# Gate logits as eight more columns of the value and output products, and a new order of the last attention steps

## The chip, the cores and the metric

The kernel runs on one core of a Trainium2 chip. The metric is the device time of one execution in microseconds. Lower is better. Nothing else runs on the chip.

## The reference

The block is linear attention followed by a mixture of experts, both on layer-normed rows with a residual. There are 4 batches of 1024 tokens, 512 features, 16 heads of 32, 8 experts with a hidden width of 2048, and each token goes to its best two experts.

```python
xn = layernorm(x)
q, k, v = xn @ q_w.T + q_b, xn @ k_w.T + k_b, xn @ v_w.T + v_b      # per head
qp, kp = elu(q) + 1, elu(k) + 1
attn = (qp @ (kp.T @ v)) / (qp @ kp.sum(tokens) + 1e-6)
x1 = x + attn @ o_w.T + o_b
x1n = layernorm(x1)
gates = softmax(x1n @ gating_w)           # 8 logits of each token
top two experts of each token, a position in each expert (cumulative count), capacity 1280
out = x1 + sum over the two experts of weight * (relu(row @ w1 + b1) @ w2 + b2)
```

## The kernel before

One core does all. The program has an attention stage, which also routes the tokens to experts, and then an expert stage. The change touches the attention stage and its seam with the first expert.

**Precision.** Most matrix products are made of three matmuls of type fp32r: both operands are split in a rounded part (`_hi`, by ACT) and a rest (`_lo`, by DVE), and hi·hi, lo·hi and hi·lo are summed. One product of a 128-row tile with a 512x512 matrix is 4 chunks of 3 matmuls of 512 columns (`product`, lines 1290 to 1300). Transposes, the gate logits, the sums over heads and the counts are plain f32 matmuls.

**Tiles and steps.** The 4096 tokens are 32 tiles of 128 rows. Every engine walks the same list of steps `t`, and step `t` works on several tiles at different stages: V and K products on tile t-3, key-value accumulation (KV) on t-4, a quarter of a query product (Q) on t-6, sums over heads (NUM) on t-13, the transpose of the attention rows (A) on t-14, the output product (O) on t-15, the transpose of the second normed rows (N) and the gate logits (L) on t-16. So steps 16 to 34 hold everything, steps 35 to 47 hold fewer and fewer parts, and from step 38 on there is neither V, K nor Q. The order of the parts within a step is written out by hand, apart for each engine: there is no scheduler. An engine that waits in its list holds up all that stands behind it.

**PE** in a full step: V, (counts of a batch, in one step of eight), transpose of xn, O, N, K, A, L, NUM, KV, Q.

**DVE** in a full step: xt_lo, (state of a batch, in one step of eight: `kvb`, `kvd`), `residual` (x1 = product + xr, its statistics), keys, at_lo, `normalize_x1` (x1n), keys_mapped, `attention` (division, writes `at`), xn and its statistics, a piece of routing in six steps of eight, queries_mapped.

**ACT** copies PSUM out (vx, the _hi parts, nt) and does the exponentials. **POOL** does the small steps of the norms (`norm_scale`: add, power), adds the output bias to the residual rows (xr) and scatters routing records to a table in DRAM, 4 indirect DMAs in a step, four steps for a batch. **SP** issues loads and stores in order; `store_rows(v)` waits for x1 and then for x1n of a tile.

**The gate logits** come from x1n: N transposes x1n, ACT copies it to `nt`, L multiplies by the 512x8 gate matrix, and `read_logits` copies the logits of 8 tiles. `route_logits`, `route_gates`, `route_choices` then choose experts; `cnt` goes to PE (`counts`), which gives positions.

**The seam.** At step 36 SP issues the eight 512 KB loads of the first expert's w1. POOL gathers the first expert's rows (`xg`) once two batches are scattered (EARLY_TABLE), PE transposes them (`rows_turned_early`), and `first_layer(0, 0, s)` starts in the last steps. first_layer(0, 0, 2) is the first matmul work behind the last step.

Of the kernel before, what the change touches and what calls it, by code (L numbers as in the profile page):

```python
# [13 lines left out]
F32 = mybir.dt.float32  # L14
# [17 lines left out]
def moe_block(nc, x_in, wq_t, bq, wk_t, bk, wv_t, bv, wo_t, bo, gate_w, w1, b1, w2, b2, out):  # L32
# [3 lines left out]
    NT = S // P  # L36
    KC = D // P
# [11 lines left out]
    ROUTE_STEPS = 36 + NT  # L49
# [14 lines left out]
    with ctx:  # L64
# [7 lines left out]
        bank = [ctx.enter_context(nc.psum_tensor(f"bank{i}", [P, 512], F32)) for i in range(8)]  # L72
# [25 lines left out]
        for c in "kv":  # L98
            whi[c], wlo[c] = sa(f"w{c}_hi", [P, KC, D], F32R), sa(f"w{c}_lo", [P, KC, D], F32R)
# [13 lines left out]
        whi["o"], wlo["o"] = sa("wo_hi", [P, KC, D], F32R), sa("wo_lo", [P, KC, D], F32R)  # L113
# [9 lines left out]
        nt = sa("nt", [P, KC, P])  # L123
# [6 lines left out]
        gw = sa("gw", [P, KC, E])  # L130
        stats = sa("stats", [P, 2, 6])
        mv = sa("mv", [P, 2, 2])
        ve = sa("ve", [P, 2])
        rstd = sa("rstd", [P, 2])
        stats2 = sa("stats2", [P, 6])
        mv2 = sa("mv2", [P, 2])
        ve2 = sa("ve2", [P, 1])
        rstd2 = sa("rstd2", [P, 1])
# [43 lines left out]
        v_full, v_done = n_("v_full"), n_("v_done")  # L182
# [9 lines left out]
        nt_full, nt_done = n_("nt_full"), n_("nt_done")  # L192
        lg_full = n_("lg_full")
        route = n_("route")
        lg_exp_in, lg_exp, lg_read = n_("lg_exp_in"), n_("lg_exp"), n_("lg_read")
# [14 lines left out]
        NTILES = B * NT  # L210
        W = P + HPG
        Z0 = 3 * R
# [11 lines left out]
        LAST_KEYS = NTILES + VK - OUT  # L224
# [18 lines left out]
        def logit_bank(b):  # L243

            return bank[5] if b < B - 1 else bank[3]

        def out_bank(v):

            return bank[7] if v < LAST_KEYS else bank[2] if v < NTILES - NT else bank[4]

# [80 lines left out]
        def _(sp):  # L331
# [36 lines left out]
            load_x(0)  # L368
            load_matrix(0, wv_t)
# [6 lines left out]
            sp.dma_start(gw[:], gate_w.rearrange("(c p) e -> p c e", p=P)).then_inc(small_landed, 16)  # L376
            with nc.allow_non_contiguous_dma(reason="512 biases"):
                sp.dma_start(bqt[:], bq.rearrange("(c p) -> p c", p=P)).then_inc(small_landed, 16)
# [67 lines left out]
        def _(pool):  # L446
# [25 lines left out]
            def norm_scale(v, done, var, tmp_, out_, step_done, ready):  # L472

                pool.wait_ge(done, v + 1)
                nc.gpsimd.tensor_scalar(tmp_, var, LN_EPS, None, ALU.add).then_inc(step_done, 1)  # L475
                pool.wait_ge(step_done, v + 1)
                nc.gpsimd.tensor_tensor(out_, tmp_, nhalf[:], ALU.pow).then_inc(ready, 1)

# [60 lines left out]
            for t in range(STEPS):  # L539
# [8 lines left out]
                if v is not None:  # L548
                    norm_scale(v, mv2_done, mv2[:, 1:2], ve2[:], rstd2[:], ve2_done, rstd2_done)
# [7 lines left out]
                if v is not None:  # L557
                    norm_scale(v, mv_done, mv[:, v % 2, 1:2], ve[:, v % 2:v % 2 + 1], rstd[:, v % 2:v % 2 + 1],
                               ve_done, rstd_done)
# [5 lines left out]
                if t == EARLY_TABLE + 1:  # L565
                    pool.wait_ge(kv_acc, NTILES)
# [47 lines left out]
        def _(act):  # L614
            def matrix_hi(m):

                for half in range(2):
                    act.wait_ge(st_landed[2 * (m % 2) + half], 16 * (m // 2 + 1))
                    nc.scalar.activation(whi[MATRICES[m]][:, 2 * half:2 * half + 2, :], matrix_half(m, half), ACT.Copy) \
# [77 lines left out]

            for t in range(STEPS):
# [5 lines left out]
                if v is not None:  # L704
                    act.wait_ge(v_full, v + 1)
                    if v >= 2:
                        act.wait_ge(kv_acc, v - 1)
                    nc.scalar.activation(vx[:, v % 2, :, 0:P], bank[2][:].rearrange("p (g c) -> p g c", g=G), ACT.Copy) \
                        .then_inc(v_done, 1)
                v = tile_at(t, TURN_X)  # L710
                if v is not None:
# [3 lines left out]
                    split_hi(bank[0], xt_hi[:, :, P * (v % NT):P * (v % NT + 1)], xt_hi_done)  # L715
                for m_ in range(KC):
# [833 lines left out]
```

## Time and profile before

| | |
|---|---|
| median of 3 runs | 2082.67 us (2082.58 to 2087.34) |
| the profiled execution | 2085.72 us |
| its span | 2084.0 us |
| PE busy | 2021.5 us, 97% |
| DVE / ACT / POOL busy | 929.9 / 598.0 / 417.3 us |
| mean granted TensorE clock | 0.99 |

The page's busy shares are averages over two stages. The attention stage ends at about 535 us of the span; the rest is the expert stage, which the change leaves as it is. The durations of single matmuls in the timeline are latencies (390 ns for 512 columns): what a matmul costs in a dense stretch is the distance from its start to the next one's.

### The profile page before, as it was taken

To read this page: it belongs to the slowest core of one execution; us is meant where nothing else is said; L and a number is where in the kernel's file an instruction comes from. 1 tells how busy PE (TensorE), PEld (TensorE's weight loads), DVE (VectorE), ACT (ScalarE), POOL (GpSimd) and SP (SyncE) were. 2 spreads that over 40 slices of the span, in tenths; PEclk is the share of its full clock that TensorE was granted. 3 is DMA by queue.
4 is the path that set the end of the run, shared out by engine and by line. 5 is a ranking of instruction groups with operands and counts; after the bars stand their busy time and mean duration, and the time that the engine had idled before them with its cause. 6 is when DMAs were issued, how large, how long until landed. Compare 5 with 4: busy or idle time off the path is not lost.

```text
span 2084.0 us, 28871 instructions
## 1 busy us (share of the span) xinstructions
PE 2021.5 (97%) x10128; PEld 1754.1 (84%) x10129; DVE 929.9 (45%) x1768; ACT 598.0 (29%) x890; POOL 417.3 (20%) x472
## 2 busy tenths in 40 slices
PE   8999999987999989999999999999999999999996
PEld 7788888876789989998998878889988988888895
DVE  5455557566842452345333432353234334334332
ACT  4333333321331341234122322232123123223221
POOL 1021113335621210221122021121120120220221
PEclk9999999998999999999999999999999999999998
DMA  7112122154202440244023321431143242232221
GB/s 199 58 58 75 64 79 72 47 172 124 75 22 41 130 98 20 40 111 116 20 40 91 101 55 19 126 87 24 32 111 96 40 110 91 45 100 92 55 40 20
DMA packets 114875, 156.05 MB, mean 75 GB/s; under 512 B 28032, under 2 KB 60928, under 8 KB 114816
## 3 DMA queue, kind: packets, MB, share of 16 engines
q1 hardware_dynamic: 93216, 112.13, 17.3%
q0 software_dynamic: 21600, 43.16, 11.5%
q8 instruction: 34, 0.56, 0.1%
q14 instruction: 25, 0.20, 0.0%
HBM read 113.15 MB, written 42.10 MB: 74 GB/s over the span
## 4 chain that ended last, share of the span: by engine, by line
PE 90%; DVE 3%; issue 2%; ACT 2%; POOL 1%; DMA 1%; SPq 1%; ACTq 0%; DVEq 0%; POOLq 0%
PE bank L1297 28%; PE bank L1299 28%; PE bank L1298 28%; PE bank L1316 2%; PE bank L1305 2%; PE bank L1482 1%; PE bank L1470 1%; PE bank L1457 1%; POOL slot_table L528 0%; SPq L385 0%; DMA xr<-_attn_hidden_states_dram 0%; DVE w_lo L838 0%; ACT w_hi L629 0%; ACT ys L646 0%; DMA xb<-_attn_hidden_states_dram 0%
## 5 line engine op out<-in xcount | busy, mean ns | idle before, releaser
L864 DVE CAST h_hi<-h 128x512 fp32r<-128x512 f32 x320 | 138.7, 433 | 846.9 <-ACT h L659 834.5
L659 ACT ACTIVATE h<-bank,b_cur 128x512 f32<-128x512 f32 x320 | 220.2, 688 | 997.6 <-PE bank L1299 965.7
L1297 PE MATMUL bank<-et_hi,w_hi 128*128 128x384 f32 (+1 forms) x1280 | 456.6, 357 | 14.6 <-issue 8.9
L1299 PE MATMUL bank<-et_hi,w_lo 128*128 128x384 f32 (+1 forms) x1280 | 455.6, 356 | 0.0
L1298 PE MATMUL bank<-et_lo,w_hi 128*128 128x384 f32 (+1 forms) x1280 | 454.4, 355 | 0.0
L1299 PE MATMUL bank<-w_hi,h_lo 128*128 128x512 f32 x1072 | 420.8, 393 | 0.0
L1297 PE MATMUL bank<-w_hi,h_hi 128*128 128x512 f32 x1072 | 420.5, 392 | 0.0
L1298 PE MATMUL bank<-w_lo,h_hi 128*128 128x512 f32 x1072 | 420.1, 392 | 0.0
L514 POOL DMA_INDIRECT out_dram<-ys,tab_s x80 | 129.1, 1613 | 1027.5 <-ACT ys L646 1009.2
L1297 PEld LDWEIGHTS bank<-et_hi,w_hi 128*128 128x128 f32 x1280 | 241.1, 188 | 43.5 <-issue 9.9
L1298 PEld LDWEIGHTS bank<-et_lo,w_hi 128*128 128x128 f32 x1280 | 240.9, 188 | 25.2 <-issue 0.2
L1299 PEld LDWEIGHTS bank<-et_hi,w_lo 128*128 128x128 f32 x1280 | 240.7, 188 | 17.5
L1299 PEld LDWEIGHTS bank<-w_hi,h_lo 128*128 128x128 f32 x1072 | 201.1, 188 | 42.7
L1298 PEld LDWEIGHTS bank<-w_lo,h_hi 128*128 128x128 f32 x1072 | 201.3, 188 | 36.8
L1297 PEld LDWEIGHTS bank<-w_hi,h_hi 128*128 128x128 f32 x1072 | 201.4, 188 | 35.8
L866 DVE TENSOR_TENSOR h_lo<-h,h_hi 128x512 fp32r<-128x512 f32 x320 | 222.1, 694 | 11.0
L496 POOL DMA_INDIRECT xg<-normed,tab_g x80 | 81.1, 1013 | 66.3 <-DMA tab_g<-slot_table 48.2
L838 DVE TENSOR_TENSOR w_lo<-w_raw,w_hi 128x1024 fp32r<-128x1024 f32 x64 | 78.0, 1219 | 3.4 <-ACT w_hi L629 3.4
L475 POOL TENSOR_SCALAR ve<-mv 128x1 f32<-128x1 f32 x64 | 14.4, 225 | 324.0 <-DVE mv L917 192.2
L844 DVE TENSOR_TENSOR w_lo<-w_raw,w_hi 128x1024 fp32r<-128x1024 f32 x64 | 78.0, 1219 | 0.0
L528 POOL DMA_INDIRECT slot_table<-rec,slot_i x64 | 72.2, 1128 | 27.6 <-issue 18.3
L850 DVE TENSOR_TENSOR et_lo<-bank,et_hi 128x512 fp32r<-128x512 f32 x84 | 54.0, 684 | 44.4 <-ACT et_hi L641 44.4
(190 smaller groups left out, 2222.9 us busy)
## 6 DMA issues: line engine op xcount, KB each, us to landing
w_raw<-L_ffn_w_dram SPq DMA_DIRECT2D x128, 512.0 KB, 3.7
xb<-_attn_hidden_states_dram SPq DMA_DIRECT2D x32, 256.0 KB, 2.7
xr<-_attn_hidden_states_dram SPq DMA_DIRECT2D x32, 256.0 KB
out_dram<-x SPq DMA_DIRECT2D x32, 256.0 KB
normed<-x1n SPq DMA_DIRECT2D x32, 256.0 KB
normed<-zrow SPq DMA_DIRECT2D x1, 2048.0 KB, 8.3
out_dram<-zrow SPq DMA_DIRECT2D x1, 2048.0 KB, 12.9
b_cur<-L_ffn_b_dram SPq DMA_DIRECT2D x8, 256.0 KB
```

The lines of the kernel that those rows point to most:

```text
L496: nc.gpsimd.indirect_dma_start(out=xg[:, h, :], out_offset=None, in_=normed, in_offset=bass.IndirectOffsetOnAxis(ap=tab_g[:, h, 0:1].bitca ...
L514: nc.gpsimd.indirect_dma_start(out=out, out_offset=bass.IndirectOffsetOnAxis(ap=tab_s[:, h, 0:1].bitcast(I32), axis=0), in_=ys[:, h, :], i ...
L528: nc.gpsimd.indirect_dma_start(out=table, out_offset=bass.IndirectOffsetOnAxis(ap=slot_i[:, c, i:i + 1], axis=0), in_=rec[:, c, i, :], in_ ...
L659: nc.scalar.activation(h32[:, mm % 2, :], h_bank[mm % 2][:], ACT.Relu, bias=b1_cur[:, mm:mm + 1]) \
L838: ve_.tensor_tensor(w1_lo[:, :, cols], w1_raw[:, :, cols], w1_hi[:, :, cols].bitcast(F32), ALU.subtract).then_inc(w1_ready, 1)
L844: ve_.tensor_tensor(w2_lo[:, two, :], w2_raw[:, two, :], w2_hi[:, two, :].bitcast(F32), ALU.subtract).then_inc(w2_ready, 1)
L850: ve_.tensor_tensor(et_lo[:, k, :], src[:], et_hi[:, k, :].bitcast(F32), ALU.subtract) \
L864: ve_.tensor_copy(h_hi[:, mm % 4, :], h32[:, mm % 2, :]).then_inc(h_split_hi, 1)
L866: ve_.tensor_tensor(h_lo[:, mm % 4, :], h32[:, mm % 2, :], h_hi[:, mm % 4, :].bitcast(F32), ALU.subtract).then_inc(h_ready, 1)
L1297: mm_(out_, lh, rh, start=(first and c == 0), stop=False)
L1298: mm_(out_, lh, rl, start=False, stop=False)
L1299: ins = mm_(out_, ll, rh, start=False, stop=(last and c == n - 1))
```

## The change

1. **V product.** The value matrix gets 8 more columns, the gate matrix. The 520 output columns lie across two PSUM banks, so each product is done as two: 268 columns and 252 columns. The second part shares its bank with the KV sums and accumulates on zeros, which ACT writes after each tile. On one step of eight PE waits for `kvb` between the two parts.
2. **O product.** Its first part shares a bank with the other half of the KV sums, so it too waits for `kvb`; where V stands ahead of it in the step, V has waited already, and only step 36 has O and a new `kvb` without V. The output matrix gets 8 columns (o_w.T times the gate matrix, worked out once on the chip in steps 9 to 11 by 16 transposes and 20 small products), 252 and 268 columns.
3. **Logits.** DVE adds the two sets of 8 columns (`lgs`), and `route_logits` corrects for mean and scale of the second norm with 5 more operations in each batch. N, the copy `nt`, L and `read_logits` go.
4. **x1n** is made by ACT instead of DVE, behind its other work of the step; POOL makes one more small operation for it and one for `std`.
5. **Order.** There is one step less; the routing steps come one step earlier. From step 37 (TAIL) on PE does NUM, A, O, and DVE does attention, at_lo, residual. `state` and `read_counts` stand at the front of DVE's step. Clearing `xg` moves from POOL to ACT.

The diff, cut to its core:

```diff
-        STATS, NORM, TURN_X, VK, KV, QUERY = 0, 1, 2, 3, 4, 6
-        RESIDUAL, NUM, TURN_A, OUT, TURN_N, LOGIT = 13, 13, 14, 15, 16, 16
-        ROUTE = NT + LOGIT
-        STEPS = NTILES + LOGIT
+        V0, O0 = 244, 260
+        KV0 = (254, 0)
+        RESIDUAL, NUM, TURN_A, OUT = 13, 13, 14, 15
+        ROUTE = NT + OUT
+        STEPS = NTILES + OUT
+        TAIL = NTILES + KV + 1
+        FRESH = TAIL - OUT
+        GATES = 9
...
 # POOL
+                    nc.gpsimd.tensor_scalar(shift2[:, one], mv2[:, v, 0:1], rstd2[:, one], -1.0, ALU.mult, ALU.mult) \
+                        .then_inc(shift2_done, 1)
...
-                    nc.gpsimd.memset(xg[:], 0.0).then_inc(xg_cleared, 1)
...
 # ACT
+            def normalize_x1(v):
+
+                act.wait_ge(shift2_done, v + 1)
+                if v >= 2:
+                    act.wait_ge(x1n_stored[v % 2], 16 * (v // 2))
+                nc.scalar.activation(x1n[:, v % 2, :], x1[:, v % 2, :], ACT.Identity, scale=rstd2[:, v:v + 1],
+                                     bias=shift2[:, v:v + 1]).then_inc(x1n_done, 1)
...
+                    nc.scalar.activation(lgx[:, v, :], pair_v[:, V0 + D:V0 + DE], ACT.Copy).then_inc(v_read, 1)
+                    act.wait_ge(v_read, v + 1)
+                    nc.scalar.activation(pair_v[:, 512:V0 + DE], zrow[:, 0:V0 + DE - 512], ACT.Copy).then_inc(v_done, 1)
...
-                    nc.scalar.activation(nt[:], bank[0][:].rearrange("p (c t) -> p c t", c=KC), ACT.Copy).then_inc(nt_done, 1)
...
 # DVE, residual
-                ve_.tensor_tensor(x1[:, v % 2, :], out_bank(v)[:], xr[:, v % RRING, :], ALU.add).then_inc(x1_done, 1)
+                ve_.tensor_tensor(x1[:, v % 2, :], pair_o[:, O0:O0 + D], xr[:, v % RRING, :], ALU.add).then_inc(x1_done, 1)
+                dve.wait_ge(std_done, v + 1)
+                ve_.scalar_tensor_tensor(out=lgs[:, v, :], in0=lgx[:, v, :], scalar=std[:, v:v + 1],
+                                         in1=pair_o[:, O0 + D:O0 + DE], op0=ALU.mult, op1=ALU.add).then_inc(lgs_done, 1)
...
 # PE
-                    product(bank[2][:], rows_, lambda k: (whi["v"][:, k, :], wlo["v"][:, k, :]), KC,
-                            matrix=0 if v == 0 else None).then_inc(v_full, 1)
+                    product(pair_v[:, V0:512], rows_,
+                            lambda k: (whi["v"][:, k, 0:512 - V0], wlo["v"][:, k, 0:512 - V0]), KC,
+                            matrix=0 if v == 0 else None)
...
+                    b = batch_at(t, KVD)
+                    if b is not None:
+                        pe.wait_ge(kvb_done, G * (b + 1))
...
+                    product(pair_v[:, 512:V0 + DE], rows_,
+                            lambda k: (whi["v"][:, k, 512 - V0:DE], wlo["v"][:, k, 512 - V0:DE]), KC, first=False,
+                            shared=True).then_inc(v_full, 1)
...
+                    if t >= KVD:
+                        pe.wait_ge(kvb_done, G * min(B, (t - KVD) // NT + 1))
+                    pe.wait_ge(at_done, min(NTILES - NT, t - NUM + (1 if t >= TAIL else 0)))
...
+                    product(pair_o[:, O0:512], out_rows,
+                            lambda k: (whi["o"][:, k, 0:512 - O0], wlo["o"][:, k, 0:512 - O0]), KC, first=(v >= FRESH),
+                            shared=True)
+                    product(pair_o[:, 512:O0 + DE], out_rows,
+                            lambda k: (whi["o"][:, k, 512 - O0:DE], wlo["o"][:, k, 512 - O0:DE]), KC).then_inc(o_full, 1)
...
-                    turn(bank[0], x1n[:, v % 2, :]).then_inc(nt_full, 1)
...
-                    for k in range(KC):
-                        ins = mm_(logit_bank(b)[:, E * i:E * (i + 1)], nt[:, k, :], gw[:, k, :], start=(k == 0),
-                                  stop=(k == KC - 1))
```

Three places show what moves. First PE around the third batch's counts, step 42 into 43 before:

```order
1667 L1298 MATMUL bank<-wo_lo,at_hi 128x512
1668 L1299 MATMUL bank<-wo_hi,at_lo 128x512
1669 L1305 MATMUL bank<-ident,x1n 128x128 x4
1670 L1305 MATMUL bank<-ident,at 128x128 x4
1671 L1457 MATMUL bank<-gw,nt 128x8 x4
1672 L1470 MATMUL bank<-kvd,qp 128x132 x4
1673 L1372 MATMUL bank<-cnt,upper 128x64
1674 L1373 MATMUL bank<-cnt,ones 128x64
1675 L1297 MATMUL bank<-wo_hi,at_hi 128x512
```

and now, step 41 into 42:

```order
2377 L1370 MATMUL pair_o<-wo_lo,at_hi 128x268
2378 L1371 MATMUL pair_o<-wo_hi,at_lo 128x268
2379 L1444 MATMUL bank<-cnt,upper 128x64
2380 L1445 MATMUL bank<-cnt,ones 128x64
2381 L1493 MATMUL bank<-kvd,qp 128x132 x3
2382 L1493 MATMUL pair_v<-kvd,qp 128x132
2383 L1377 MATMUL bank<-ident,at 128x128 x4
2384 L1369 MATMUL pair_o<-wo_hi,at_hi 128x252
```

The transposes of x1n and the logits are gone, and the counts stand directly behind the O product of the step whose choices they count.

Second DVE at the state of the second batch (step 20), before:

```order
209 L985 SCALAR_TENSOR_TENSOR qp<-bank,bq_one,qe 128x512
210 L832 TENSOR_TENSOR xt_lo<-bank,xt_hi 128x4x128
211 L924 COPY ks<-bank 128x2 x2
212 L927 SCALAR_TENSOR_TENSOR kvb<-bvb,ks,bank 128x128 x4
213 L934 TENSOR_TENSOR kvd<-kvb,headmask 128x4x128
```

and now:

```order
222 L1041 SCALAR_TENSOR_TENSOR qp<-bank,bq_one,qe 128x512
223 L985 COPY ks<-pair_v 128x2
224 L985 COPY ks<-pair_o 128x2
225 L988 SCALAR_TENSOR_TENSOR kvb<-bvb,ks,pair_v 128x128 x2
226 L988 SCALAR_TENSOR_TENSOR kvb<-bvb,ks,pair_o 128x128 x2
227 L995 TENSOR_TENSOR kvd<-kvb,headmask 128x4x128
```

`kvb` moved ahead of xt_lo, behind the queries of the step before; PE now waits for it in the middle of V.

Third ACT in steps 40 to 43, as it stands now (x1n is what moved here from DVE, gt is the exponential of the gates):

```order
322 L660 ACTIVATE w_hi<-w_raw 128x4x256
323 L746 ACTIVATE gt<-gt 128x64
324 L656 ACTIVATE at_hi<-bank 128x512
325 L739 ACTIVATE x1n<-x,shift,rstd 128x512
326 L656 ACTIVATE at_hi<-bank 128x512
327 L739 ACTIVATE x1n<-x,shift,rstd 128x512
```

Each at_hi, the split of a later tile's attention rows, stands behind the x1n of an earlier tile, which waits for DVE's statistics and POOL.

## Rows read from the trace of the kernel before

**Rows 1.** The page: busy time of the engines.

```profile
PE 2021.5 (97%) x10128; PEld 1754.1 (84%) x10129; DVE 929.9 (45%) x1768; ACT 598.0 (29%) x890; POOL 417.3 (20%) x472
```

**Rows 2.** Windows of the attention stage; the first row names the columns.

```profile
core 0: us, PE busy (x) PEld busy (x) DVE busy (x) ACT busy (x) POOL busy (x), PEclk, DMA share, GB/s
...
250.00:300.00 50.00, 50.00 (x283) 42.88 (x282) 27.73 (x64) 15.38 (x27) 9.48 (x17) 1.00 0.20 64
450.00:500.00 50.00, 35.26 (x197) 29.31 (x196) 31.25 (x85) 7.84 (x14) 32.16 (x36) 0.84 0.62 162
```

**Rows 3.** Timeline, PE, one full step: start us, us, engine, line, op, operands, count.

```profile
274.89 0.39 PE L1297 MATMUL bank<-wv_hi,xt_hi 128*128 128x512 f32 x1
...
275.57 0.39 PE L1297 MATMUL bank<-wv_hi,xt_hi 128*128 128x512 f32 x1
...
280.81 0.60 PE L1305 MATMUL bank<-ident,x1n 128*128 128x128 f32 x4
281.16 0.47 PE L1297 MATMUL bank<-wk_hi,xt_hi 128*128 128x512 f32 x1
...
281.93 0.40 PE L1297 MATMUL bank<-wk_hi,xt_hi 128*128 128x512 f32 x1
...
284.44 0.96 PE L1457 MATMUL bank<-gw,nt 128*128 128x8 f32 x8
285.26 1.15 PE L1470 MATMUL bank<-kvd,qp 128*128 128x132 f32 x8
286.24 1.06 PE L1482 MATMUL bank<-vx,kp 128*128 128x129 f32 x8
...
289.88 0.39 PE L1297 MATMUL bank<-wv_hi,xt_hi 128*128 128x512 f32 x1
```

**Rows 4.** Timeline, PE, expert stage: 384 columns, three matmuls from row to row.

```profile
1000.00 0.33 PE L1297 MATMUL bank<-et_hi,w_hi 128*128 128x384 f32 x1
...
1000.52 0.33 PE L1297 MATMUL bank<-et_hi,w_hi 128*128 128x384 f32 x1
```

**Rows 5.** Timeline, PE and DVE, step 20 (state of the second batch).

```profile
199.96 0.39 PE L1297 MATMUL bank<-wv_hi,xt_hi 128*128 128x512 f32 x1
...
201.54 0.75 DVE L985 SCALAR_TENSOR_TENSOR qp<-bank,bq_one,qe 128x512 f32<-128x512 f32 x1 [1.82 <-ACT qe L749]
...
204.62 0.21 DVE L924 COPY ks<-bank 128x2 f32<-128x2 f32 x2
204.87 1.12 DVE L927 SCALAR_TENSOR_TENSOR kvb<-bvb,ks,bank 128x128 f32<-128x128 f32 x4
```

**Rows 6.** Timeline, PE's V and DVE's first counts (step 27).

```profile
304.87 0.39 PE L1297 MATMUL bank<-wv_hi,xt_hi 128*128 128x512 f32 x1
...
306.57 0.22 DVE L1078 TENSOR_TENSOR cnt<-oh 128x64 f32<-128x64 f32 x1
```

**Rows 7.** Timeline, PE: steps 36, 39 and 43, and first_layer(0, 0, 2).

```profile
435.71 0.39 PE L1297 MATMUL bank<-wo_hi,at_hi 128*128 128x512 f32 x1
...
463.96 0.77 PE L1297 MATMUL bank<-wo_hi,at_hi 128*128 128x512 f32 x1 [4.79 <-DVE at_lo L832]
...
500.02 0.66 PE L1372 MATMUL bank<-cnt,upper 128*128 128x64 f32 x2 [7.73 <-DVE cnt L1078]
...
534.80 0.48 PE L1297 MATMUL bank<-et_hi,w_hi 128*128 128x512 f32 x1
```

**Rows 8.** Timeline, DVE: kvb of the fourth batch, residual of tiles 21 and 23.

```profile
438.28 1.12 DVE L927 SCALAR_TENSOR_TENSOR kvb<-bvb,ks,bank 128x128 f32<-128x128 f32 x4
...
440.14 0.69 DVE L947 TENSOR_TENSOR x<-bank,xr 128x512 f32<-128x512 f32 x1
...
461.65 0.69 DVE L947 TENSOR_TENSOR x<-bank,xr 128x512 f32<-128x512 f32 x1 [6.24 <-DMA out_dram<-x]
```

**Rows 9.** Timeline, POOL: the first work of steps 38 and 39.

```profile
462.19 1.26 POOL L545 TENSOR_TENSOR xr<-xr,bob 128x512 f32<-128x512 f32 x1 [7.10 <-DMA xr<-_attn_hidden_states_dram]
...
469.69 1.29 POOL L545 TENSOR_TENSOR xr<-xr,bob 128x512 f32<-128x512 f32 x1
```

More of the change, by code:

```diff
@@ L1044, in route_logits @@
                 step, k = stepper(b, 0)
+                tiles = slice(NT * b, NT * (b + 1))
+                over = lambda which: gate_sums[:, E * which:E * (which + 1)].unsqueeze(1).to_broadcast([P, NT, E])
+                dve.wait_ge(lgs_done, NT * (b + 1))
+                dve.wait_ge(rstd2_done, NT * (b + 1))
+                step(ve_.tensor_tensor(dm[:], mv[:, tiles, 0], mv2[:, tiles, 0], ALU.subtract))
+                step(ve_.tensor_tensor(lg[:], over(0), wide(dm[:]), ALU.mult))
+                step(ve_.tensor_tensor(lg[:], lg[:], over(1), ALU.add))
+                step(ve_.tensor_tensor(lg[:], lg[:], lgs[:, tiles, :], ALU.add))
+                step(ve_.tensor_tensor(lg[:], lg[:], wide(rstd2[:, tiles]), ALU.mult))
                 step(ve_.tensor_reduce(col(RM), lg[:], AX.X, ALU.max))
@@ L1158, in _ @@
                 v = tile_at(t, OUT)
-                if v is not None:
-                    normalize_x1(v)
+                if v is not None and t >= TAIL:
+                    residual(v)
                 v = tile_at(t, VK)
@@ L1164, in _ @@
                 v = tile_at(t, NUM)
-                if v is not None:
+                if v is not None and t < TAIL:
                     attention(v)
@@ L1288, in warm, with product @@
                     mm_(bank[6][:, 0:P], ident[:], ident[:], start=True, stop=True)
-            def product(out_, left, right, n, first=True, last=True, matrix=None):
+            def product(out_, left, right, n, first=True, last=True, matrix=None, shared=False):
                 for c in range(n):
@@ L1371, in counts @@
                 c2 = cnt[:].rearrange("p t e -> p (t e)")
[L1372 to L1382 removed]
+                mm_(cum_bank(b)[:, 0:R], upper[:], c2, start=True, stop=True)
@@ new lines, in attention_rows, with sums @@
+            def attention_rows(t):
+                v = tile_at(t, TURN_A)
+                if v is not None:
+                    pe.wait_ge(at_done, v + 1)
+                    if v >= 1:
+                        pe.wait_ge(att_lo_done, v)
+                    turn(bank[7], at[:, v % 2, :]).then_inc(att_full, 1)
+            def sums(t):
+                v = tile_at(t, NUM)
+                if v is not None:
+                    b = v // NT
+                    half = v // 4
+                    pe.wait_ge(kvd_done, 2 * (b + 1))
+                    pe.wait_ge(qp_done, KC * (half + 1))
+                    if v == 0:
+                        pe.wait_ge(sums_read, 1)
+                    else:
+                        pe.wait_ge(at_done, v)
+                    if t >= OUT and v < NTILES - NT:
+                        pe.wait_ge(lgs_done, t - OUT + (1 if t < TAIL else 0))
+                    for g in range(G):
+                        q_ = qp[:, q_slot(half), g, P * (v % 4):P * (v % 4 + 1)]
+                        dst = bank[6][:, W * g:W * (g + 1)] if g < G - 1 else z_cols(v)
+                        ins = mm_(dst, q_, kvd[:, b % 2, g, :], start=True, stop=True)
+                    ins.then_inc(num_full, 1)
@@ L1408, in _ @@
                     turn(bank[0], xn[:, v % 2, :]).then_inc(xt_full, 1)
+                if t == GATES:
+                    for c in range(KC - 1):
+                        gate_turn(c)
+                if t == GATES + 1:
+                    gate_turn(KC - 1)
+                if t == GATES + 2:
+                    gate_products()
+                if t >= TAIL:
+                    sums(t)
+                    attention_rows(t)
                 v = tile_at(t, OUT)
```

289 lines of the change are left out of this document (156 added, 133 removed).

## The prediction, made before the change was run

> **What bounds the kernel now.** I read the page's busy line first: PE 97% [rows 1]. That is a mean over two stages, so next the windows: at 250 to 300 us PE is busy for 50.00 of 50 us at full clock, but at 450 to 500 us for only 35.26, at a granted clock of 0.84 [rows 2]. So the attention stage has two parts. In its body (to 435.71 us, where step 36 begins) PE is the bound, and an instruction on it costs its distance to the next. In its tail (435.71 to 534.80 us [rows 7]) PE waits, and what counts is the chain it waits for. The timeline of one step gives the distances: V to V is 289.88 - 274.89 = 14.99 us [rows 3]. In the tail the timelines of PE, DVE and POOL show three brakes: DVE waited 6.24 us for the store of x1 [rows 8], held up behind the w1 loads; POOL takes 7.50 us for a step with scatters (462.19 to 469.69) [rows 9]; PE waited 7.73 us for the counts' input [rows 7].
>
> **Part 1, what goes in the body.** N: 281.16 - 280.81 = 0.35 us, and the first K matmul behind it takes 0.77 us for three where 0.68 is usual (275.57 - 274.89), so 0.43 with the change of kind. L: 285.26 - 284.44 = 0.82 [rows 3]. Together 1.25 us a tile. Twenty tiles (steps 16 to 35) have it in the body: **-25.0 us**. PE is full there, so it counts whole.
>
> **Part 2, the longer products.** No fp32r matmul of 252 or 268 columns stands in the trace. 512 columns take 0.68/3 = 227 ns, 384 columns 0.52/3 = 173 ns [rows 3, 4]: 0.42 ns a column and some 13 ns fixed. On that line 252 and 268 columns are 118 and 125 ns, 243 for the pair against 227: 16 ns, by 12 pairs 0.19 us a product. The lower end is the pure column cost, 8 columns x 0.42 x 12 = 0.04 us. The upper end is plain f32: NUM makes 4 matmuls of 132 columns in 0.98 us (286.24 - 285.26), 245 ns each and 468 ns for 252 columns, 0.35 more for each. I take the line, since the two fp32r rows are of the same kind. The weight load is no floor at 118 ns: the 8 instructions of L, whose streams are next to nothing, stand 0.82/8 = 102 ns apart, each with its load. In the body there are 32 V and 21 O products: 53 x 0.19 = **+10.1 us**. TensorE: Matmul & The Clock Gate of the Trainium skill (Back-to-back issue gap) gives N/2.4 + 2.5 ns, so 2.5 ns fixed, not 13: by it the pair would cost 6 ns more instead of 16, and the sum over all 64 products would be some 7.7 us lower. The rows disagree: 227 ns for 512 columns against its 216.
>
> **Part 3, what is new in the body.** The gate matrix through o_w: 16 transposes at 0.35/4 and 20 products of two instructions at 102 ns, 1.4 + 4.1 = **+5.5 us**, once. The split of its parts ahead of the first V and a small load ahead of the value matrix: **+0.6 us** (between 0.2, two small operations, and 2). The wait for kvb: the queries begin 1.58 us after V (201.54 - 199.96) and take some 0.7; ks and kvb then need 0.25 + 1.12, so kvb is there 3.65 us after V's start. The first part of V ends at 12 x 125 ns = 1.5. PE stands **2.15 us, in steps 12, 20 and 28** [rows 5]; behind it wait the transpose of xn and all of PE's step. One wait of 0.9 us for kvd goes: +5.5 us. The counts: cnt ends 1.92 us after V's start [rows 6]. The first V part takes 1.5, and DVE has kept its place relative to K while PE reaches this point about 0.8 us sooner by losing L: 1.25 us in steps 26 and 34, less a wait of 0.6 that goes, **+1.9 us**. lgs, the zeroing, x1n on ACT and the ACT copies lie in gaps of DVE (27.73 of 50 us busy) and ACT (15.38) [rows 2]: nothing, because NUM and KV come 3 us behind the end of O and DVE needs about 1.3 for x1, lgs and the zeros. If that cover were gone it would be up to 1 us a step.
>
> Body: -25.0 + 10.1 + 5.5 + 0.6 + 5.5 + 1.9 = **-1.4 us**. The gain and the price nearly cancel.
>
> **Part 4, the tail.** I follow the chain from step 36. From x1 of tile 21 (440.14 to 440.83) to residual(23) it is 20.8 us by the loads of 4 MB ahead of the store [rows 8]; that stays. But x1 of tile 21 comes later in its step. Before, O ran beside DVE's state of the fourth batch, and x1 ended 5.12 us into step 36 (440.83 - 435.71). Now O waits for kvb, which ends at 438.28 + 1.12 = 439.40: PE stands 3.7 us, O takes 3.0, x1 0.7, and it ends 7.6 us into the step. **+2.5 us** for all behind it, and 0.5 for a matmul or two at half clock: **+3.0 us**. Call S the point where POOL goes on, 462.19 before [rows 9]. Before, first_layer(0, 0, 2) starts at S + 72.6 and the third counts at S + 37.8 [rows 7]. Now:
> - POOL has two scatter rounds left instead of three, each step 7.5 + 0.3 for the new operation = 7.8 us, no clearing of xg. The norms of tiles 24, 25, 26 are there at S + 10.3, 18.2, 23.5, the last gather is issued at S + 28 and lands some 4 us later.
> - ACT's x1n waits for them, and at_hi of the next step behind it: at_hi(27) at S + 19.5, at_lo(27) 20.3. DVE then has residual(26) with its statistics (1.75) and the choices (2.3): cnt at S + 24.4. PE, whose bare step is NUM 0.9, A 0.43, O 3.0 = 4.35 us, stands there some 5 to 9 us. This is the wait that takes the place of the one removed.
> - Behind it: two steps of 4.35, and about 1.5 us for the half clock after such a wait. x1n(28) waits for residual(28), and with it the split of the gathered rows on ACT: the transposes of xg are done at S + 43, O(30) at S + 49, first_layer 0 at 53, O(31) 56, first_layer 1 at 59.
> - relu(0, 0) is behind x1n(31) on ACT, and that behind POOL's scatter round: first_layer(0, 0, 2) at **S + 63**.
>
> So from S on the tail gives 72.6 - 63 = 9.6 us back; with the +3.0 it is **-6.6 us**. Its bounds: if PE's 4.35 us ruled each step, S + 51 (-21.6 for that part); if POOL's and DVE's chains kept their pace of before, S + 72 (-0.6). I take the value between, because each link above is a wait in an order that is written out.
>
> **Part 5, behind the seam.** hidden(0, 0) and the splits of w1 and w2 start with relu(0, 0), now at the start of first_layer(0, 0, 2) and not 2.5 us ahead of it, and DVE has 5 more operations of about 0.25 us in the last route_logits: **+1.2 us**. The expert loops are unchanged.
>
> **Sum**: -1.4 - 6.6 + 1.2 = -6.8 us on the profiled execution: span 2084.0 to 2077.2, time 2085.72 to 2078.9. That execution lies 3 us above the median of the runs; against the median it is 2082.67 - 6.8, so **2076 us**.
>
> **Rivals.**
> - *The tail's waits only change their names.* x1n on ACT ties at_hi of each step to POOL, and POOL's step gets longer. For it: POOL was the slowest in these steps (7.50 us [rows 9]). Against: one scatter round less remains behind S. Behind S the tail then gives 0 to 3 us, and the time is 2082 to 2085 (2082.67 - 1.4 + 3.0 + 1.2, less 0 to 3).
> - *PE rules the tail.* If POOL and ACT keep up within the two steps of slack that the order gives, first_layer(0, 0, 2) is at S + 51 and the time 2076 - 12 = 2064. Against: the count above finds four waits on the way.
> - *Narrow fp32r matmuls lose their speed* (the other side). The 252-column ones run at f32's pace, 0.35 us more for each: 12 x 64 x 0.35 = +269 us, less the 7 of the forecast, about 2345 us. From 9 ns more on each of the 768 it costs more than the change brings. For it: no fp32r matmul under 384 columns is in the trace. Against: 384 and 512 lie on one line, and L's spacing shows no slow load.
> - *More waits in the body.* The kvb wait, the counts and DVE's longer steps cost twice what I count, +9 us, and the tail behind S gives half of its 9.6: 2076 + 9 + 4.8 = 2090.
>
> **How the numbers follow.** My forecast with its neighbourhood (2070 to 2081) 0.44; PE rules the tail 0.18; only names change 0.20; more waits 0.10; narrow matmuls slow 0.08. This kernel can be told from no change at about 0.3%, 6.2 us, so the line is 2076.4. Faster by more: the second case whole and 0.31 of the first, 0.49. Within: 0.13 of the first and the third whole, 0.33. Slower: the last two, 0.18. The range, 2060 to 2089, leaves out the slow narrow matmuls, half of "more waits" and the outer part of the second case. The likeliest case's own range is 2070 to 2081.
>
> **What would show it.** A full step of 14.1 to 14.2 us in the body. Spacings of 118 and 125 ns in V and O. Waits of about 2 us in the middle of V in steps 12, 20, 28. Step 36 beginning 1 to 2 us earlier than 435.71, no more, and a wait of 3.7 us before its O. In the tail a PE wait of 5 to 9 us for cnt, and ACT's at_hi behind x1n behind POOL. first_layer(0, 0, 2) at about 527. Wrong would be: 252 columns over 135 ns apart, a body that ends before 430 or after 440, or a tail in which PE waits under 3 us in all.

## The result, and the profile after

The changed kernel takes 2115.55 us (median of 4 runs, 2108.42 to 2117.8) against 2085.01 us of the kernel before, run beside it (2082.58 to 2088.74): a ratio of 1.0139, 95% interval 1.0108 to 1.017. It is **slower by some 30 us**; I had forecast 2076, and a range that ended at 2089. The profiled execution of the changed kernel took 2108.42 us, its span is 2106.8, so 22.8 us more than the span before.

Where are they? First the page of the changed kernel: the span, the busy line that answers to [rows 1], and the instruction queue.

```profile
span 2106.8 us, 29878 instructions
...
PE 2012.8 (96%) x10568; PEld 1779.3 (84%) x10569; DVE 923.0 (44%) x1811; ACT 621.9 (30%) x961; POOL 429.1 (20%) x535
...
q8 instruction: 70, 1.15, 0.2%
```

PE is busy 8.7 us less and yet ends 22.8 us later. The queue that fetches instructions carried 70 packets. Before, the same line of the page had half of that:

```profile
q8 instruction: 34, 0.56, 0.1%
```

The second look is at the seam. first_layer(0, 0, 2), at 534.80 us before [rows 7], is at 534.07 now. So the attention stage gives 0.7 us, and the whole loss lies behind it, in the loops that the diff does not touch. PE's timeline of the kernel before, at five places where a loop over tiles ends or an If is not taken, so where PE jumps (in brackets PE's idle time ahead, and what ended it; a row without brackets had none), and one wait behind the third of them:

```profile
763.36 0.69 PE L1297 MATMUL bank<-et_hi,w_hi 128*128 128x384 f32 x1 [5.31 <-issue]
...
1202.50 0.49 PE L1297 MATMUL bank<-et_hi,w_hi 128*128 128x512 f32 x1 [2.38 <-issue]
...
1607.95 0.34 PE L1297 MATMUL bank<-et_hi,w_hi 128*128 128x384 f32 x1
...
1613.57 0.44 PE L1297 MATMUL bank<-et_hi,w_hi 128*128 128x384 f32 x1 [1.26 <-ACT h L659]
...
1766.98 0.33 PE L1297 MATMUL bank<-et_hi,w_hi 128*128 128x384 f32 x1
...
1926.01 0.33 PE L1297 MATMUL bank<-et_hi,w_hi 128*128 128x384 f32 x1
```

The same five jumps in the changed kernel:

```profile
763.86 0.68 PE L1369 MATMUL bank<-et_hi,w_hi 128*128 128x384 f32 x1 [5.03 <-issue]
...
1207.52 0.79 PE L1369 MATMUL bank<-et_hi,w_hi 128*128 128x512 f32 x1 [6.67 <-issue]
...
1619.69 0.68 PE L1369 MATMUL bank<-et_hi,w_hi 128*128 128x384 f32 x1 [4.35 <-issue]
1620.17 0.52 PE L1370 MATMUL bank<-et_lo,w_hi 128*128 128x384 f32 x1
1620.49 0.52 PE L1371 MATMUL bank<-et_hi,w_lo 128*128 128x384 f32 x1
...
1783.97 0.68 PE L1369 MATMUL bank<-et_hi,w_hi 128*128 128x384 f32 x1 [4.02 <-issue]
...
1948.31 0.68 PE L1369 MATMUL bank<-et_hi,w_hi 128*128 128x384 f32 x1 [4.25 <-issue]
```

Four waits for "issue" are longer: 6.67 us for 2.38, and 4.35, 4.02 and 4.25 us where PE had not waited at all, 16.9 us together. The kernel before has three waits of 1.26 us for ACT's h, each 5.6 us behind one of the last three jumps (1613.57, 1772.59 and 1931.62). They are gone, since h is there by then: 3.8 us back, so 13.1 us. "issue" says that PE waited for nothing that the profile shows. What it waited for is seen in the instruction queue. From 1190 us to the end of the span the kernel before has no packet on it; in the changed kernel the DMA view of that window (1190 to 2106.8 us) has

```profile
q8 instruction: 33, 0.54, 0.3%
```

and 3 of them lie between 1195 and 1210 us, around the wait of 6.67 us. So PE fetched instructions again that it had run in the loops already. Behind each wait the matmuls stand 0.32 us apart (1620.17 to 1620.49), not 0.17 [rows 4], at the lower of the two clocks, 1.2 GHz (granted 0.50, the third figure from the end):

```profile
1620.20:1625.20 5.00, 5.00 (x17) 5.00 (x16) 0.43 (x2) 1.27 (x2) 4.08 (x4) 0.50 0.85 145
```

From the first of these places to the end it is 1342.9 us now (2106.8 - 763.86) and 1320.6 before: 22.3 us, of which 13.1 are the waits and the other 9.2 the slow clock behind them, some 2.3 us each. Windows from 560 to 700 us are equal in both traces (140.00 us busy of 140), so the matmuls of the loops themselves did not get slower.

In the attention stage the page of the body reads as forecast at first. A full step (PE, V to V, then two spacings of 268 columns):

```profile
267.69 0.28 PE L1369 MATMUL pair_v<-wv_hi,xt_hi 128*128 128x268 f32 x1
...
281.64 0.28 PE L1369 MATMUL pair_v<-wv_hi,xt_hi 128*128 128x268 f32 x1
281.76 0.29 PE L1370 MATMUL pair_v<-wv_lo,xt_hi 128*128 128x268 f32 x1
...
282.01 0.29 PE L1369 MATMUL pair_v<-wv_hi,xt_hi 128*128 128x268 f32 x1
```

A step takes 13.95 us where it took 14.99 [rows 3]. What eats this is in the steps that wait (kvb of step 28, the counts of step 26, kvb of step 36):

```profile
298.60 0.41 PE L1444 MATMUL bank<-cnt,upper 128*128 128x64 f32 x2 [1.35 <-DVE cnt L1137]
...
330.52 0.39 PE L1369 MATMUL pair_v<-wv_hi,xt_hi 128*128 128x252 f32 x1 [3.34 <-DVE kvb L988]
...
331.44 0.28 PE L1370 MATMUL pair_v<-wv_lo,xt_hi 128*128 128x252 f32 x1
331.55 0.33 PE L1371 MATMUL pair_v<-wv_hi,xt_lo 128*128 128x252 f32 x1
331.68 0.41 PE L1369 MATMUL pair_v<-wv_hi,xt_hi 128*128 128x252 f32 x1
331.89 0.41 PE L1370 MATMUL pair_v<-wv_lo,xt_hi 128*128 128x252 f32 x1
...
441.22 0.55 PE L1369 MATMUL pair_o<-wo_hi,at_hi 128*128 128x252 f32 x1 [3.71 <-DVE kvb L988]
```

The 252-column matmuls stand 0.11 to 0.12 us apart up to 331.55 and 0.21 from 331.68 on: again half clock (granted 0.50 from 331.7 to 333.5), 1.2 us after a wait of 3.34. Step 36 begins at 441.22 - 3.71 = 437.5 (435.71 before [rows 7]).

### The profile page after: what moved, and what is told of

The parts are those of the page before. It is cut to its first block, busy times and chain, and to the rows that moved or that the text cites. A ratio compares the mean times of both kernels' runs of the same rounds, so it can differ in the third digit from the quotient of the medians.

```text
span 2106.8 us, 29878 instructions
## 1 busy us (share of the span) xinstructions
PE 2012.8 (96%) x10568; PEld 1779.3 (84%) x10569; DVE 923.0 (44%) x1811; ACT 621.9 (30%) x961; POOL 429.1 (20%) x535
## 3 DMA queue, kind: packets, MB, share of 16 engines
q8 instruction: 70, 1.15, 0.2%
## 4 chain that ended last, share of the span: by engine, by line
PE 90%; DVE 3%; issue 3%; ACT 1%; DMA 1%; POOL 1%; SPq 1%; ACTq 0%; POOLq 0%; DVEq 0%
PE bank L1369 17%; PE bank L1370 16%; PE bank L1371 16%; PE pair_v L1369 7%; PE pair_v L1370 7%; PE pair_v L1371 7%; PE pair_o L1371 5%; PE pair_o L1370 5%; PE pair_o L1369 5%; PE bank L1377 1%; PE pair_v L1388 1%; PE bank L1493 1%; PE pair_o L1388 1%; PE pair_o L1587 1%; PE pair_v L1587 1%
## 5 line engine op out<-in xcount | busy, mean ns | idle before, releaser
L1369 PE MATMUL bank<-w_hi,h_hi 128*128 128x512 f32 x752 | 296.5, 394 | 0.0
L1370 PE MATMUL bank<-w_lo,h_hi 128*128 128x512 f32 x752 | 295.0, 392 | 0.0
L1371 PE MATMUL bank<-w_hi,h_lo 128*128 128x512 f32 x752 | 294.8, 392 | 0.0
L1369 PE MATMUL bank<-et_hi,w_hi 128*128 128x384 f32 (+1 forms) x640 | 233.8, 365 | 31.7 <-issue 25.3
L1371 PE MATMUL bank<-et_hi,w_lo 128*128 128x384 f32 (+1 forms) x640 | 232.0, 363 | 0.0
L1370 PE MATMUL bank<-et_lo,w_hi 128*128 128x384 f32 (+1 forms) x640 | 231.6, 362 | 0.0
L1369 PE MATMUL pair_v<-et_hi,w_hi 128*128 128x384 f32 (+1 forms) x640 | 228.2, 357 | 0.0
L1371 PE MATMUL pair_v<-et_hi,w_lo 128*128 128x384 f32 (+1 forms) x640 | 227.9, 356 | 0.0
L1370 PE MATMUL pair_v<-et_lo,w_hi 128*128 128x384 f32 (+1 forms) x640 | 227.6, 356 | 0.0
L1370 PEld LDWEIGHTS bank<-w_lo,h_hi 128*128 128x128 f32 x752 | 141.5, 188 | 22.9
L1369 PEld LDWEIGHTS pair_v<-et_hi,w_hi 128*128 128x128 f32 x640 | 121.2, 189 | 12.8
```

The lines of the kernel that those rows point to most:

```text
L1369: mm_(out_, lh, rh, start=(first and c == 0), stop=False, skip_group_check=shared)
L1370: mm_(out_, lh, rl, start=False, stop=False, skip_group_check=shared)
L1371: ins = mm_(out_, ll, rh, start=False, stop=(last and c == n - 1), skip_group_check=shared)
```

## The experiments

**Does the place of the loops in PE's program matter?** The packets on the instruction queue are 16.4 KB (1.15 MB in 70). I took each for a block of 256 instructions of 64 bytes, the size that they have in the built program; after_256 tests this, as it moves the loops by a whole block. One edit, on either kernel: N instructions more at PE's start.

```
             pe.sem_inc(et_full, 1)
+            for _ in range(2 * N):          # two waits make one instruction
+                pe.wait_ge(et_full, 1)
             pe.wait_ge(const_done, 3)
```

> The kernel before with 75 instructions more on PE ahead of everything (waits on a semaphore that has long been reached; they run in the first 3.7 us, in which PE waits anyway). Nothing else is changed. Theory (placement): the loops over experts have the same instructions, but fetching PE's instructions at the jumps depends on where the loops lie in its program; the blocks fetched are 16.4 KB (0.56 MB in 34 packets), 256 instructions of 64 bytes. By my count the loop nest begins at PE instruction 5880 before and at 6979 after the change, 248 and 67 beyond a multiple of 256; 75 more put it at 67 as well. Then the instruction queue carries about 66 to 70 packets instead of 34, the waits put down to 'issue' at 1202, 1613, 1772 and 1931 us grow from 2.4, 0, 0, 0 to some 6.7, 4.3, 4.0, 4.3, each with about 2 us of half clock behind it, and the time is 2085 + 22 = 2107, up to 2112. Rival (the bank names, the stores of x or the routing data of the changed kernel disturb the loops): none of that is here, so 2085 and 34 packets. Rival (the longer program costs in itself, not its place): 75 instructions are 1% of it, 2085 to 2087.

> The changed kernel with 128 such instructions more on PE at its start; nothing else is changed. Theory (placement): the loop nest of 1608 instructions then begins half a block of 256 further on, and lies in one block fewer of those that the fetch keeps; packets on the instruction queue fall from 70 to about 38, the four 'issue' waits at the ends of the experts' tiles go back to those of the kernel before (one of about 5 us at 764, at most 2.4 elsewhere), and the time is 2115 less 22 = 2090 to 2093 by the medians, the profiled span 2084 to 2086. Rival (banks, or a longer program): 2115 to 2118, with 70 packets or more.

> The changed kernel with 256 such instructions more. Theory (placement, with blocks of 256): the same place within a block as the changed kernel itself, so the same waits, about 70 packets and 2115 us (up to 3 us more if the added instructions outlast PE's first wait). Rival (what counts is the distance from the start, or any shift helps): near 2090, as with 128.

Measured: before_75 2092.09 us (ratio to before 1.0035, 1.0017 to 1.0053), after_128 2097.15 (1.006, 1.0043 to 1.0077), after_256 2141.97 (1.0261, 1.0238 to 1.0285). In the changed kernel the theory holds: with 128 the new waits are gone, with 256 they are back. before_75 was a miss (2107 expected, with 66 to 70 packets; it has 37). I had counted a plain f32 matmul as one pair of instructions; its rows stand twice in the trace (128 in the program, x256 on the page), so before_75 had moved the nest to another place than I wrote. The added instructions were not free either: the first V begins at 11.27 us in the changed kernel, at 21.78 in after_128 and at 35.88 in after_256. The second 128 cost 14.1 us, 110 ns each; the first 128 show only 10.5, because PE waited 3.7 us there anyway. That is why the times of after_128 and after_256 lie above what was expected (2090 to 2093, and 2115): take the later start away and they are 2086.6 and 2117.4.

**The same with a block that is jumped over**, and so costs almost nothing, in both kernels:

```
+            with pe.Fori(0, 2) as never:
+                with pe.If(never * never - never > 0):
+                    for _ in range(256):
+                        pe.wait_ge(et_full, 1)
```

> The kernel before, with a block of 128 instructions on PE that is jumped over at its start, and so costs almost no time; with the jump it is 135 more. Recounted (a plain f32 matmul stands for two matmuls, each with its load) the loop nest is 1608 instructions long and begins at PE instruction 6696 in the kernel before, 7579 after the change, that is 40 and 155 past a multiple of 256; before_75 has 115 (37 packets, no new waits in the loops), after_128 27 (38 packets) and after_256 155 again (74 packets, the waits back). Theory: what decides is whether the nest touches 7 or 8 blocks of 256, with an edge between 115 and 155. Here it begins at 175: about 70 packets, the waits for 'issue' at the ends of the experts' tiles as in the changed kernel (6.7, 4.3, 4.0, 4.2 us) though no other line is changed, and 2085 + 21 = 2106 us. Rival (the place matters only in the changed kernel, through its banks or its waits): 2085 to 2088, some 35 packets.

> The changed kernel with the same jumped-over block; its loop nest begins at 34. Theory (placement): after_128 without the 10.5 us that its waits took at the start, so 2097 - 10.5 = 2087 us, 38 packets: with the placement made good the change is worth nothing, within 0.3% of the kernel before, since the attention stage gives 0.7 us back where I had forecast 8. Rival (part of the 30 us is in something else than placement): 2092 or more.

Measured: before_skip128 **2104.73 us** (1.01, 1.0083 to 1.0118), after_skip128 **2088.03 us** (1.0013, 1.0004 to 1.0023). Both as the theory says. The kernel before, with not one executed line of its work changed, shows the new waits (PE's timeline of before_skip128):

```profile
1202.84 0.79 PE L1301 MATMUL bank<-et_hi,w_hi 128*128 128x512 f32 x1 [6.79 <-issue]
...
1613.68 0.68 PE L1301 MATMUL bank<-et_hi,w_hi 128*128 128x384 f32 x1 [3.19 <-issue]
...
1941.90 0.68 PE L1301 MATMUL bank<-et_hi,w_hi 128*128 128x384 f32 x1 [3.02 <-issue]
```

And the changed kernel, moved, has lost them (after_skip128, the second and third jump):

```profile
1205.48 0.49 PE L1373 MATMUL bank<-et_hi,w_hi 128*128 128x512 f32 x1 [2.36 <-issue]
...
1610.95 0.33 PE L1373 MATMUL bank<-et_hi,w_hi 128*128 128x384 f32 x1
...
1616.56 0.44 PE L1373 MATMUL bank<-et_hi,w_hi 128*128 128x384 f32 x1 [1.26 <-ACT h L690]
```

All seven, with where the nest of 1608 instructions begins, past a multiple of 256 (a count from the built programs), the packets of q8, and the time from the end of the first wait at the loops (763.36 before) to the end of the span:

| kernel | begins at | packets | loops, us |
|---|---|---|---|
| after_128 | 27 | 38 | 1320.2 |
| after_skip128 | 34 | 38 | 1320.4 |
| before | 40 | 34 | 1320.6 |
| before_75 | 115 | 37 | 1321.1 |
| the changed kernel | 155 | 70 | 1342.9 |
| after_256 | 155 | 74 | 1343.4 |
| before_skip128 | 175 | 67 | 1342.3 |

Two levels, 22 us apart, and the place alone decides between them, in either kernel; the jumped-over block doesn't, since it stands in a kernel of each level. 1608 is 6 blocks and 72 instructions; a nest that begins late in a block touches one block more. By plain arithmetic the edge is at 184 (256 - 72); the runs put it between 115 and 155. What shifts it by 29 to 69 instructions was not tried. One thing would fit: the count leaves out the labels of the built program (34 to 38 ahead of the nest, 9 in it). If they are fetched like instructions, the nest is 1613 long, begins at 60 to 148 in the four quick kernels and at 188 to 211 in the three slow ones, and the edge by arithmetic is at 179, between the two. No run shows whether it is so.

The Trainium skill, Runtime: NRT & Kernel Launch (Instruction fetch mechanics), says that instructions come in blocks of 256, that PE has room for 2048, and that a taken branch to a block outside the window stalls for a fetch. The 16.4 KB packets agree with the first. A nest that stays resident in seven blocks but not in eight would fit the second if one block is kept for fetching ahead, which no run tests. The third is what the waits of 3.0 to 6.9 us above look like. The same section speaks of a window of two blocks; in this trace PE goes back over 1608 instructions without a fetch (no packet behind 1190 us in the kernel before), so for PE that does not hold. The section's rule on branches is the one that bears on this change, and my prediction didn't weigh it.

**What the new order of the last steps is worth.** after_skip128, with the body's order on PE and DVE from step 37 on (the edit in short):

```
-                if t >= TAIL:                  # PE; likewise on DVE and in the waits
+                if t >= STEPS:
                     sums(t)
                     attention_rows(t)
```

> As after_skip128, but PE and DVE keep the order of the body in the last steps too (step 37 on: transposes of the attended rows, sums, V's place, output; on DVE attention behind the residual). Everything else of the change is in. If the new order is what lets the tail gain (forecast: two steps of slack, part of my -9.6 us) first_layer(0, 0, 2) comes 4 to 12 us later than in after_skip128 and the time is 2091 to 2099. Rival (the waits only change their names; POOL's and ACT's steps rule): 2085 to 2089, the same as after_skip128.

Measured: 2087.98 us (1.0014, 1.0005 to 1.0023), against 2088.03 with the new order. The rival is right: the order is worth nothing. Call S, as in the prediction, the point where POOL goes on; from S to first_layer(0, 0, 2) it is 65.7 us in both (468.18 to 533.92, 471.08 to 536.73). The waits of PE only have other names: 6.93 us before O and 6.33 for cnt in the one, 4.27, 4.50 and 4.00 before O, the sums and cnt in the other.

**What the waits for kvb cost.** after_skip128, with this work put between in the steps of a batch's state (the edit in short):

```
+                if late and t < OUT:            # step 12
+                    keys_product()
+                    second_half()               # V's upper columns
...
+                    if late:                    # steps 20, 28, 36
+                        upper_part()            # O's 268 columns, another bank
+                        if tile_at(t, VK) is not None:
+                            second_half()
```

> As after_skip128, but in the steps in which a batch's state is made (12, 20, 28, 36), the second part of V and the first part of O, which share banks with what DVE reads there and wait for kvb, are made later: in step 12 the key product goes ahead of the second part of V, in steps 20, 28 and 36 O's upper 268 columns go ahead of it. Theory (the kvb wait costs its length and then some 2 us of half clock: steps 20 and 28 took 17.83 and 19.11 us where 13.95 is usual): 3.7 + 3.7 + 3.5 us come back in the body and 1.5 to 2 in step 36, 2087 - 11 = 2076 us. Rival (the steps behind absorb it, since the norms of x or DVE then set the pace): 2083 to 2087.

Measured: **2076.59 us** (0.9961, 0.9948 to 0.9975), 11.4 less than after_skip128, and faster than the kernel before. Against after_skip128 step 12 takes 12.86 us instead of 13.94 (with two new waits of 1.22 and 0.86), step 20 14.31 instead of 16.24, step 28 15.61 instead of 19.09; that is 6.5 us, and 4 more come from step 36, since S is 10.8 us earlier (460.32 instead of 471.08). So the sum was right, but its shares (3.7, 3.7, 3.5 and 1.5 to 2) were not. PE's waits that are left:

```profile
329.50 0.38 PE L1373 MATMUL pair_v<-wv_hi,xt_hi 128*128 128x252 f32 x1 [1.40 <-DVE kvb L988]
...
436.61 0.35 PE L1373 MATMUL pair_o<-wo_hi,at_hi 128*128 128x252 f32 x1 [2.13 <-DVE kvb L988]
...
524.48 0.76 PE L1373 MATMUL bank<-et_hi,w_hi 128*128 128x512 f32 x1 [4.27 <-ACT h L690]
```

**Is x1n on ACT the brake of the tail?** In the last of those rows PE waits for a relu on ACT, which stands behind the last x1n, which waits for POOL (after_skip128_upper):

```profile
522.55 0.81 ACT L739 ACTIVATE x1n<-x,shift,rstd 128x512 f32<-128x512 f32 x1 [4.94 <-POOL shift L580]
...
523.65 0.69 ACT L690 ACTIVATE h<-bank,b_cur 128x512 f32<-128x512 f32 x1 [0.18 <-ACT b_cur L683]
```

Three kernels, all on top of after_skip128_upper: upper_relu does relu(0, 0) ahead of the last x1n; upper_x1n does every x1n one step later, behind at_hi; upper_x1n_order is that with the body's order.

```
                     split_hi(bank[7], at_hi[:, v % 2], att_hi_done)
+                v = tile_at(t, OUT + 1)         # upper_x1n
+                if v is not None:
+                    normalize_x1(v)
```

> As after_skip128_upper (2076.6 us), but on ACT the first relu of the expert stage stands ahead of the last x1n, not behind it. Where first_layer(0, 0, 2) now waits 4.27 us for this relu, x1n(31) waits 4.94 us for POOL's shift behind its scatters. Theory: that one place is worth 3 to 4 us, 2073 us. Rival: the splits of w1 and w2, counts and records of the last batch behind it set the time anyway, 2075 to 2077.

> As after_skip128_upper, but x1n of every step stands on ACT behind the split at_hi of the next step, and the last one behind the first relu; so nothing that PE waits for stands behind a scatter of POOL. Theory (what took the tail's gain is x1n ahead of at_hi: in steps 39 to 44 at_hi ends 0.6 us behind x1n, and x1n 0.7 us behind POOL's shift): the waits of 3.2, 2.5, 4.5 us there shrink, first_layer(0, 0, 2), now at 524.5, comes 8 to 14 us earlier, and the time is 2063 to 2069. Rival (DVE's route work and the wait for cnt, or the store of x behind the w1 loads, rule the tail): first_layer(0, 0, 2) gains only the 4 us of the last step, 2071 to 2074.

> As upper_x1n, but with the body's order in the last steps. In after_skip128_order that order cost nothing. Theory (the new order gives two steps of slack, which the chain over POOL and ACT used up; with the chain cut the slack is worth something): 3 to 8 us slower than upper_x1n. Rival (the order never matters): the same as upper_x1n within 2 us.

Measured: upper_relu **2073.38 us** (0.995, 0.9938 to 0.9962), 3.2 less: as the theory says, and the fastest kernel of this study. These three ran at another time than after_skip128_upper; by the ratios to the kernel before, which ran beside both, the gain is 2.3 us, and the spans of the two profiled executions lie 1.6 apart. upper_x1n 2084.39 (1.0007, 0.9997 to 1.0017), 7.8 **more** than after_skip128_upper (9.6 by the ratios): neither of my two expectations. upper_x1n_order 2085.98 (1.0012, 1.0003 to 1.002), 1.6 more than that, so the rival is right; the order hardly matters here either. One place where upper_x1n loses is SP's queue, where the store of x1n stands ahead of the next load of xr and the w1 loads. In after_skip128_upper, issues on SP:

```profile
435.12 0.32 SPq L383 DMA_DIRECT2D normed<-x1n  x1
439.01 0.33 SPq L369 DMA_DIRECT2D xr<-_attn_hidden_states_dram  x1
```

and in upper_x1n:

```profile
445.38 0.32 SPq L383 DMA_DIRECT2D normed<-x1n  x1
445.75 0.43 SPq L369 DMA_DIRECT2D xr<-_attn_hidden_states_dram  x1
```

The xr load goes out right behind the late store, 6.7 us later, and S is 6.6 us later (POOL: 466.90 instead of 460.32). But these rows show the end of the loss, not where it arose. PE begins step 36 already 5.3 us later (439.80 instead of 434.48), though it began step 12 1.9 us earlier. It loses in three places of the body: step 26 takes 18.2 us instead of 16.0, step 28 17.9 instead of 15.6, and steps 34 and 35 together 27.3 instead of 24.6. Two waits are longer in the body: DVE's for ACT's `ke`, 1.19 us instead of 0.49, and from 395 us on POOL's for the xr load (4.82 us at 413.01 instead of 0.50 at 406.10; earlier some 1.6 in both). That the later x1n loses time ahead of step 36 is shown, by which of these links is not. From S on, first_layer(0, 0, 2) comes after 59.4 us (526.25), after 60.3 in upper_relu (459.73 to 520.03), and after 64.2 in after_skip128_upper. So cutting at_hi from POOL's chain was worth about 1 us behind S beyond what upper_relu gives, and its price ahead of S was 6.6. The link that I had counted step by step is there in the trace, but it hardly brakes anything.

## Why the prediction was wrong

**The step that failed: "The expert loops are unchanged", costed at nothing.** The instructions are the same, but PE's program ahead of them grew by 883 instructions, which moved the nest from 40 to 155 past a block's start. That is 22.3 of the 22.8 us between the spans. before_skip128 and after_skip128 show it in both directions. I had seen how the change moves instructions on each engine, and the "issue" waits of 5.31 and 2.38 us at the loops' jumps, and put the two together nowhere. The rivals didn't have it either. Without it the forecast would have missed as well: the attention stage gave 0.7 us, not 8.0, and the seam took 1.2, so the spans would still differ by +0.5 us, not by -6.8 (after_skip128 measured a ratio of 1.0013). That miss is in Parts 3 and 4 below.

**Part 1 and 2, the body's plain step: right, a little better.** 13.95 us where 14.1 to 14.2 were forecast; 0.12 and 0.12 to 0.13 us for 252 and 268 columns. The line through 512 and 384 columns holds below 384. The rival of slow narrow matmuls is out.

**Part 3, what is new in the body: two of three waits right, the price of each too low.** Forecast were 2.15 us in steps 12, 20 and 28; measured 2.03, 2.03 and 3.34. But step 20 is 3.9 us longer than a plain one (17.83 - 13.95) and step 28 5.2 (19.11 - 13.95): behind the wait come another 1.8 us in each, at half clock (only 0.3 in step 20 of after_skip128: 16.24 - 13.95 - 2.02). I had priced that in the tail only. Why the wait of step 28 is 1.2 us longer than forecast is open. The counts cost 2.0 us in step 26 and nothing in step 34 (forecast 1.9 for both). The gate products cost more than their own 4.4 us as well: steps 9 to 11, which hold them and the transposes, took 8.3 us longer than before, where I had 5.5 and some 0.6 for the longer V:

```profile
94.89 1.04 PE L1464 MATMUL bank<-gw,ones 128*128 128x16 f32 x8
95.78 0.48 PE L1369 MATMUL bank<-wk_hi,xt_hi 128*128 128x512 f32 x1
...
96.49 0.63 PE L1371 MATMUL bank<-wk_hi,xt_lo 128*128 128x512 f32 x1
96.92 0.63 PE L1369 MATMUL bank<-wk_hi,xt_hi 128*128 128x512 f32 x1
...
99.74 0.40 PE L1370 MATMUL bank<-wk_lo,xt_hi 128*128 128x512 f32 x1
```

After 4.4 us of matmuls with 8 and 16 columns the key product runs 0.43 us apart instead of 0.23 for some 3.4 us (granted clock 0.50 from 96.5 to 99.4), though PE never stood still. In all, step 36 begins 1.8 us later than before, where I had 1.4 earlier.

**Part 4, the tail: -2.5 us for -6.6.** Ahead of S I had +3.0 and it is +5.4 (S is 31.9 us into step 36, 26.5 before [rows 7, 9]). The wait for kvb is exactly the forecast 3.7 us, but O behind it ran at half clock and x1 of tile 21 ended 8.95 us into the step, not 7.6 (my own terms, 3.7 + 3.0 + 0.7, give 7.4). From there to S it is 22.9 us, 21.4 before; I had left that stretch unchanged, and why it grew by 1.5 is open:

```profile
445.77 0.69 DVE L1008 TENSOR_TENSOR x<-pair_o,xr 128x512 f32<-128x512 f32 x1 [3.98 <-PE pair_o L1371]
```

From S on I had 63 us and it is 64.7 (469.37 to 534.07), 72.6 before:

```profile
469.37 1.28 POOL L574 TENSOR_TENSOR xr<-xr,bob 128x512 f32<-128x512 f32 x1 [5.99 <-DMA xr<-_attn_hidden_states_dram]
...
494.56 0.41 PE L1444 MATMUL bank<-cnt,upper 128*128 128x64 f32 x2 [4.01 <-DVE cnt L1137]
...
534.07 0.77 PE L1369 MATMUL bank<-et_hi,w_hi 128*128 128x512 f32 x1 [4.21 <-ACT h L690]
```

The wait for cnt was 4.0 us, not 5 to 9. The size of this term was nearly right (7.9 for 9.6), but in part by luck: the order of the last steps, to which I gave two steps of slack, is worth nothing (after_skip128_order). Of the 7.9 us that did come, a scatter round less behind S is the likeliest source, by POOL's 7.5 us for such a step [rows 9]; this was not tried alone.

**Part 5, the seam: right.** +1.2 us forecast; 763.86 - 534.07 is 229.8 us, against 228.6 before.

**What stays open.** The four runs of the changed kernel spread over 9 us (2108.42 to 2117.8), and the profiled one is the fastest, so the medians lie 30 us apart and the spans 22.8; after_skip128 spreads over 5. It fits waits for a fetch that differ from run to run, but no run shows that. At the first jump into the loops PE waited 5.0 to 5.7 us in ten of the twelve kernels and 15.21 and 14.79 in before_75 and after_256. The instruction queue carried two packets at that jump in the ten and five in these two, so the long wait is for more fetches; why there are more is open, and the place in a block does not explain it, since the changed kernel has after_256's place and waited 5.03.

## What to carry to other kernels

An engine whose loop nest is about as long as the instructions that it keeps (here seven blocks of 256 on PE) pays for where that nest lies: before crediting or blaming a change, compare the instruction queue's packets and the "issue" waits at the jumps, and move the loop with a block that is jumped over (here 22 us for 135 instructions). A wait of 2 us or more on a full PE can cost up to twice its length (2.03 us of waiting, 3.9 in all), for the half clock behind it; filling it with work on another bank gave 11.4 us, more than the change itself was meant to bring. And a link that can be seen in the trace is not yet a brake: the chain over x1n was there at each step, and cutting it gained 1 us behind S and cost 6.6 ahead of it, in loads and copies that I hadn't looked at.

## What the runs showed of the hardware

- The instruction fetch: 16.4 KB a packet; a nest of 1608 PE instructions fetched either once or again on every pass (34 to 38 packets, or 67 to 74), in the second case PE waited 3.0 to 6.9 us at a jump, with some 2.3 us of half clock behind it (22.3 us in all in the changed kernel).
- An instruction that only waits for semaphores long reached costs PE 110 ns (14.1 us for 128, after_256 against after_128).
- The granted clock also fell to half without any idle time, behind 40 matmuls of 8 and 16 columns in 4.4 us (0.79 in the window 96 to 104 us, 0.50 from 96.5 to 99.4).
- fp32r matmuls of 252 and 268 columns stand 0.12 us apart, on the line of the longer ones, each with its own weight load.
